# Cross-attention and quantised feed-forward on one core: earlier normalisation, q tiles, output passes and input scaling, and the last shares by products

## The chip, the cores and the metric

The kernel runs on one core of a Trainium2 chip. The metric is device time in microseconds (us). TensorE is called PE below, VectorE DVE, ScalarE ACT, GpSimd POOL, and SP is SyncE's queue, from which every DMA of this kernel is issued.

## The reference, cut to what matters

There are 16 sequences of 256 tokens and 512 features, 16 heads of 32 features, and one layer:

```python
x = x + xattn(layernorm(x), ctx, ctx, wq, wk, wv, wo_w, wo_b)
x = x + ffn(layernorm(x), W_in, b_in, W_out, b_out)

# xattn: q from the normalised x, k and v from ctx; rope on q and k
qp, kp, vp = rope(q @ wq.T), rope(k @ wk.T), v @ wv.T
scores = where(|i - j| <= 128, qh @ kh.T * sqrt(32), -inf)
out = (softmax(scores) @ vh) @ wo_w.T + wo_b
# ffn: W_in and W_out rounded to 8 bit by row, x and hidden to 16 bit by one scale over the tensor
out = quant16(gelu(quant16(x) @ quant8(W_in) + b_in)) @ quant8(W_out) + b_out
```

## The kernel before, in words

There are three stages. Stage A (0 to about 761 us of the span) is the attention, one step for each of the 16 sequences b. Stages B and C (to the end) are the two feed-forward products; the change leaves them alone. Their 16-bit scale needs the maximum over all of x, so B starts only when A has ended.

All five queues carry hand-written orders in which nothing is reordered at run time; semaphores tie them. Stage A is software-pipelined: step b holds the attention of sequence b, the projections of b+1, the output product, residual and moments of b-1, and the first layer norm's moments of b+2. `has_o`, `has_proj` and `has_xt` say which of these exist; all do in steps 2 to 13.

**First half of a step.** PE computes the scores of 16 heads in pairs (L597, two matmuls a head, two banks in turn). A head's scores wait until DVE has taken the row maxima of the head before last (`row_maxima`, L1063). After each pair comes a projection tile, listed in `tiles`: k half 0; the transposes of x (L526) and k half 1; v of the first 128 tokens; q half 0; q half 1; and v of the second 128 tokens in two halves. On DVE, after each pair, comes what `between` lists: `invert` (the reciprocal of the softmax denominators of b-1, L1104) after pair 0; `xt_rest`; the rotations of k; and `normalise` (L1110) after pair 5, which multiplies the attention output oT of b-1 with the reciprocals. These have to be spread over partitions first: SP sends them to a scratch tensor in HBM and back (`spread_shares`, L349 and L352), and the second transfer signals `share_in`. The transposes of x write the bank that holds the denominators, so they wait for `den_done` of `invert` as well as for `ln1_norm`, which ACT gives after scaling x by the layer norm in place (`norm1`, L820).

**Second half.** DVE negates and splits the maxima (`split_max`, L1068), PE transposes them (L609, once a step), ACT copies them into `q_st` (`max_copy`), and SP copies them on for heads 4 to 15 (`stack_max`). PE then computes transposed scores head by head (L631), ACT takes exp (L864), POOL zeroes what is outside the window (`band`, L1381). Between these heads PE places the 24 matmuls ("passes", L581) of the output product of b-1. After heads 7, 11 and 15, and once more at the end, PE runs a clump: 4 heads' product with v (L645) and their denominators (L658). Transposed scores use three banks, so head 15 waits for the exp of head 12. The next step starts with L597 behind the last clump.

Beside that, ACT splits q and the context into a high part (`split_hi`, `ctx_hi`), POOL computes the low parts (L1358, L1364) between its bands of heads 4 to 11, and DVE does, in this order: `split_max`, the rotations of q, residual and moments of the first half of b-1, `quantise_win` (the rounding of 128 rows of W_in, L1116 to L1123), `ln1` of b+2 (L1024 to L1037, of which 13 instructions work on 2 elements a partition), residual and moments of the second half, and two maxima (`largest`, L1049). SP loads the next rows of W_in (`load_win(b+1)`, L326) when `quantise_win(b)` has ended; behind it in its queue stand the context's load, four groups of stacking DMAs, the store of x1, then the load of x and `spread_shares` of the next step.

Of the kernel before, what the change touches and what calls it, by code (L numbers as in the profile page):

```python
# [20 lines left out]
ALU = mybir.AluOpType  # L21
AX_X = mybir.AxisListType.X
F32 = mybir.dt.float32
# [6 lines left out]
P = 128  # L30
NB, S, D = 16, 256, 512
H, DK = 16, 32
# [32 lines left out]
def constants():  # L65
# [10 lines left out]
    mask = np.concatenate([mask[P:], mask[:P, P:]], 1)  # L76
    hot = np.tile((np.arange(HOT) % NC4 == NC4 - 1).astype(np.float32), (P, 1))
    sel = np.zeros((P, H), np.float32)
    for h in range(H):
        sel[MROW + h, h] = sel[MROW + H + h, h] = 1.0  # L80
    return {"c_rope": rope, "c_mask": mask, "c_sel": sel, "c_hot": hot, "c_ident": np.eye(P, dtype=np.float32)}


def build(nc, t):
# [12 lines left out]
    with ExitStack() as ctx:  # L97
# [22 lines left out]
        for n in ("wk", "wq", "wv", "wo"):  # L120
# [17 lines left out]
        oT = sb("oT", [P, NC4, S], F32, pa)  # L138
        hot = sb("hot", [P, HOT], F32, pa)
        x_ln = sb("x_ln", [P, 2, D], F32, pa)  # L140
        x_res = sb("x_res", [P, 2, D], F32, pa)
# [54 lines left out]

        c_in, rope_in, ident_in, b_out_in = sem("c_in"), sem("rope_in"), sem("ident_in"), sem("b_out_in")
        w_in = {n: sem("in_" + n) for n in ("wk", "wq", "wv", "wo")}
# [16 lines left out]
        st_mm, exp_done, p_ready, pv_mm = sem("st_mm"), sem("exp_done"), sem("p_ready"), sem("pv_mm")  # L215
        den_mm, den_done, den_out, share_in, oT_out, onorm = (
            sem(n) for n in ("den_mm", "den_done", "den_out", "share_in", "oT_out", "onorm"))
        xres_b, res_done = sem("xres_b"), sem("res_done")
# [86 lines left out]
        def _(sp):  # L305
# [33 lines left out]
            def stack_max(b):  # L339

                sp.wait_ge(mT_done, MAX_COPIES * (b + 1))
                for i in range(1, NC4):
                    sp.dma_start(q_st[MROW:P, KC * i:KC * (i + 1)].bitcast(F32),
                                 q_st[MROW:P, 0:KC].bitcast(F32)).then_inc(max_stacked[i - 1], 16)

# [51 lines left out]
            for i in range(2, NC4):  # L397
                stack_part("q", i, 0, part_hi)
                stack_part("q", i, 1, part_hi)
                stack_part("q", i, 2, part_lo)  # L400
            load_ctx(2)

            def step(b, has_o, has_proj, has_xt, has_next):
# [27 lines left out]
            for b in range(NB - 4, NB):  # L431
# [4 lines left out]
                step(b, True, b + 1 < NB, b + 2 < NB, b + 3 < NB)  # L436
            spread_shares(NB - 1)
            load_xres(NB - 1)
# [71 lines left out]
        def _(pe):  # L510
# [189 lines left out]
            def step(b, par, has_c, has_o, has_proj, has_xt):  # L700

                tiles = [[] for _ in range(H // 2)]
                if has_proj:
                    tiles[0] += [lambda: qk_tile(b + 1, "k", 0)]
                    tiles[1] += [lambda: x_transposes(b + 1, 0), lambda: x_transposes(b + 1, 1), lambda: qk_tile(b + 1, "k", 1)]
                    tiles[2] += [lambda: v_tile(b + 1, 0)]
                    tiles[3] += [lambda: qk_tile(b + 1, "q", 0)]
                    tiles[4] += [lambda: qk_tile(b + 1, "q", 1)]
                    tiles[5] += [lambda: v_tile(b + 1, 1, range(2))]
                    tiles[6] += [lambda: v_tile(b + 1, 1, range(2, KC))]  # L710
# [15 lines left out]
                some(4)  # L726
                for n, count in enumerate((1, 2, 2, 3, 1, 1, 1, 0, 1, 1, 1, 0, 1, 1, 0, 0)):
                    scores_t(b, n, has_o, has_proj)
                    some(count)
                    if n in (7, 11, 15):  # L730
                        clump(b, par, n // KC - 1, has_proj)
# [3 lines left out]

            steps(pe, step)
            for _ in o_products(NB - 1, False):
                pass
# [65 lines left out]
        def _(act):  # L804
# [86 lines left out]
            v_copy(0, 0, 1)  # L891
            ctx_hi(1)

            def step(b, par, has_c, has_o, has_proj, has_xt):
                if has_proj:
                    norm1(b + 1)
                if has_proj:
                    xt_lead(b + 1, 0)
                    xt_lead(b + 1, 1)
                    v_copy(b + 1, 1 - par, 0)  # L900
                    split_hi("k", b + 1)
                if has_o:
                    ot_lead(b - 1, 0, has_proj)
                    ot_lead(b - 1, 1, has_proj)
                if has_proj:
                    v_copy(b + 1, 1 - par, 1)
                max_copy(b, 0, slice(0, 2))
                max_copy(b, 0, slice(2, KC))
                for n in range(H):
                    softmax_exp(b, n)  # L910
                    if n == 4 and has_proj:
                        split_hi("q", b + 1)
                    if n == 8 and has_xt:
                        ctx_hi(b + 2)
                    if n == 12:
                        oT_copy(b, 0)
                    if n == 13 and has_o:
                        centre(b - 1, 0)
                if has_o:
# [101 lines left out]
        def _(dve):  # L1021
# [151 lines left out]
            def step(b, par, has_c, has_o, has_proj, has_xt):  # L1173

                between = {p: [] for p in range(H // 2)}
                if has_o:
                    between[0] += [lambda: invert(b - 1)]
                    between[5] += [lambda: normalise(b - 1, 0), lambda: normalise(b - 1, 1)]
                if has_proj:
# [12 lines left out]
                if has_o:  # L1192
                    residual(b - 1, 0)
                    ln2_moments(b - 1, 0)
                quantise_win(b)
                if has_xt:
                    ln1(b + 2)
                if has_o:
                    residual(b - 1, 1)
# [10 lines left out]
            invert(NB - 1)  # L1210
            normalise(NB - 1, 0)
            normalise(NB - 1, 1)
            ot_rest(NB - 1, 0)
# [242 lines left out]
```

## Time and profile before

| | us |
|---|---|
| median of 3 runs | 1254.26 (1252.21 to 1255.16) |
| the profiled execution | 1251.07 |
| its span | 1249.3 |
| PE busy | 1138.1 (91%) |
| DVE busy | 981.0 (79%) |
| ACT busy | 639.6 (51%) |
| POOL busy | 366.4 (29%) |

The span is the stretch that the profile covers; 1.8 us of the execution lie around it. Busy time is summed over instructions, and matmuls overlap, so PE's share overstates its work. The chain of work that ended last runs 38% over PE, 31% over DVE, and 24% is issue time.

### The profile page before, as it was taken

How to read it: one execution, taken by the hardware profiler on the slowest of the kernel's cores; microseconds unless marked ns; L12 is line 12 of the kernel's file. 1: busy time of each engine (PE TensorE's matmuls, PEld its weight loads, DVE VectorE, ACT ScalarE, POOL GpSimd, SP SyncE). 2: the span in 40 equal slices, each digit the busy share in tenths (PEclk: the TensorE clock that was granted, in tenths of full speed). 3: DMA queues.
4: the chain of work that ended last, by engine and by line, in shares of the span. 5: the costliest groups of instructions: out<-in, count | busy, mean ns of one | idle time of the engine just before them, and what ended most of it. 6: DMA issues, size and time to landing. Idle time of an engine off the chain costs nothing.

```text
span 1249.3 us, 23318 instructions
## 1 busy us (share of the span) xinstructions
PE 1138.1 (91%) x7776; PEld 759.7 (61%) x7776; DVE 981.0 (79%) x2527; ACT 639.6 (51%) x1000; POOL 366.4 (29%) x540
## 2 busy tenths in 40 slices
PE   5889999999999899999999665999999979999997
PEld 5767777787777688677768443444444434444443
DVE  6769989989988988988899545666666678888885
ACT  5254355335435534543553243555655458777774
POOL 1136336344533634453363220000000030112220
PEclk9889999999999999999999787999999989999999
DMA  8453575566456447545644711455554400567762
GB/s 270 110 143 106 158 178 137 139 183 155 108 161 177 131 134 194 140 120 164 177 119 114 218 56 69 160 206 198 208 188 143 152 0 35 186 224 249 219 207 92
DMA packets 96055, 191.44 MB, mean 153 GB/s; under 512 B 13392, under 2 KB 24912, under 8 KB 95952
## 3 DMA queue, kind: packets, MB, share of 16 engines
q1 hardware_dynamic: 95952, 190.14, 51.5%
q8 instruction: 56, 0.92, 0.3%
q14 instruction: 47, 0.39, 0.1%
HBM read 89.43 MB, written 44.04 MB: 107 GB/s over the span
## 4 chain that ended last, share of the span: by engine, by line
PE 38%; DVE 31%; issue 24%; DMA 3%; SPq 2%; ACT 2%; POOL 0%; DVEq 0%; ACTq 0%; POOLq 0%
PE bank L792 17%; DVE bank L1063 6%; PE bank L514 4%; PE bank L515 4%; PE bank L516 4%; DVE bn L1024 3%; PE bank L597 2%; DVE roped L1089 2%; DVE neg_max L1104 2%; DVE rt L1086 2%; DVE row_max L1063 2%; DVE rt L1087 2%; DVE x_res L1056 1%; PE bank L526 1%; PE bank L581 1%
## 5 line engine op out<-in xcount | busy, mean ns | idle before, releaser
L1063 DVE CUSTOM_DVE_ANT_0 bank<-bank,mask 128x256 f32<-128x256 f32 x512 | 201.4, 454 | 54.6 <-PE bank L597 48.0
L792 PE MATMUL bank<-wout_int,g_hi 128*128 128x512 bf16 x512 | 195.8, 382 | 8.8 <-DVE g_lo L1336 8.7
L792 PE MATMUL bank<-wout_int,g_lo 128*128 128x512 bf16 x512 | 195.6, 382 | 0.0
L761 PE MATMUL bank<-qT_hi,win_int 128*128 128x512 bf16 x512 | 194.2, 379 | 1.4 <-DVE qT_lo L1254 1.4
L761 PE MATMUL bank<-qT_lo,win_int 128*128 128x512 bf16 x512 | 194.1, 379 | 0.0
L864 ACT ACTIVATE probs<-bank 128x512 f32<-128x512 f32 x256 | 142.4, 603 | 52.8 <-PE bank L631 48.3
L1381 POOL TENSOR_SCALAR_AFFINE_SELECT probs<-probs 128x256 f32<-128x256 f32 x256 | 109.1, 430 | 82.9 <-ACT probs L864 78.6
L1336 DVE TENSOR_TENSOR g_lo<-h_int,g_hi 128x512 f16<-128x512 f32 x128 | 104.3, 815 | 35.6 <-ACT g_hi L991 34.3
L597 PE MATMUL bank<-k_st,q_st 96*128 96x256 f32 x512 | 98.4, 306 | 25.7 <-DVE row_max L1063 19.3
L1374 POOL TENSOR_TENSOR x_res<-x_res,wo_b 128x512 f32<-128x512 f32 x32 | 42.0, 1332 | 243.9 <-DMA x_res<-in_x 231.1
L964 ACT ACTIVATE h_ring<-bank,b_in,g_scale 128x512 f32<-128x512 f32 x96 | 73.5, 778 | 75.2 <-PE bank L761 58.1
L1278 DVE TENSOR_REDUCE hmax<-h_ring 128x512 f32 (+1 forms) x96 | 63.4, 682 | 60.6 <-ACT h_ring L964 58.6
L631 PEld LDWEIGHTS bank<-q_st,k_st 128*128 128x128 f32 x512 | 90.3, 193 | 31.8 <-issue 13.6
L597 PEld LDWEIGHTS bank<-k_st,q_st 96*128 96x128 f32 x512 | 76.8, 195 | 50.1 <-DVE row_max L1063 30.8
L631 PE MATMUL bank<-q_st,k_st 128*128 128x256 f32 x512 | 104.1, 294 | 3.1 <-DMA q_st<-q_st 2.0
L991 ACT CAST g_hi<-h_int 128x512 f16<-128x512 f32 x128 | 78.7, 615 | 39.6 <-PE bank L792 31.4
L792 PEld LDWEIGHTS bank<-wout_int,g_hi 128*128 128x128 f16 x512 | 50.4, 98 | 71.4 <-issue 11.2
L1421 POOL TENSOR_TENSOR xq<-xq,b_out 128x512 f32<-128x512 f32 x32 | 48.3, 1540 | 154.5 <-DMA xq<-x_scratch 147.7
L761 PEld LDWEIGHTS bank<-qT_hi,win_int 128*128 128x128 bf16 x512 | 50.1, 98 | 62.3 <-DVE qT_lo L1254 3.1
L792 PEld LDWEIGHTS bank<-wout_int,g_lo 128*128 128x128 f16 x512 | 50.4, 98 | 61.0 <-issue 1.6
L761 PEld LDWEIGHTS bank<-qT_lo,win_int 128*128 128x128 bf16 x512 | 50.1, 98 | 59.2
L514 PE MATMUL bank<-cT_hi,wk_hi 128*128 128x256 f32 x256 | 74.5, 291 | 12.6 <-DVE cT_lo L1141 12.6
(146 smaller groups left out, 2666.2 us busy)
## 6 DMA issues: line engine op xcount, KB each, us to landing
hidden_scratch<-h_ring SPq DMA_DIRECT2D x96, 256.0 KB, 2.0
h_ring<-hidden_scratch SPq DMA_DIRECT2D x96, 256.0 KB, 3.0
k_st<-k_hi SPq DMA_DIRECT2D x128, 128.0 KB, 2.5
q_st<-q_hi SPq DMA_DIRECT2D x128, 128.0 KB, 2.4
xq<-x_scratch SPq DMA_DIRECT2D x16, 1024.0 KB, 6.2
x_ln<-in_x SPq DMA_DIRECT2D x16, 512.0 KB, 4.5
ctx_raw<-in_ctxT SPq DMA_DIRECT2D x16, 512.0 KB, 4.9
k_st<-k_lo SPq DMA_DIRECT2D x64, 128.0 KB, 2.7
```

Source lines behind the costliest of these rows:

```text
L514: pe.matmul(out, l_hi, r_hi, start=first, stop=False)
L597: mm = pe.matmul(ring[n % 2][:, qb * S:(qb + 1) * S], q_st[0:MROW, n, qb * P:(qb + 1) * P], k_st[0:MROW, n], start=True, stop=True)
L631: mm = pe.matmul(third[n][:, kb * S:(kb + 1) * S], k_st[:, n, kb * P:(kb + 1) * P], q_st[:, n], start=True, stop=True)
L761: mm = pe.matmul(bank[f % 4][:], win_int[:, c, f * P:(f + 1) * P], part[:, par, c], start=c == 0 and part is qT_hi, stop=c == KC - 1 and p ...
L792: mm = pe.matmul(bank[4 * par + u][:], part[:, f % 4, u * P:(u + 1) * P], wout_int[:, f], start=f == 0 and part is g_hi, stop=f == FC - 1 ...
L864: act.activation(probs[:, n % SLOTS].rearrange("p k q -> p (k q)"), third[n][:], ACT.Exp, scale=SCORE_SCALE).then_inc(exp_done, 1)
L964: act.activation(dst, bank[f % 4][:], ACT.Gelu, bias=b_in[:, f:f + 1], scale=g_scale[:, f:f + 1]).then_inc(gelu_done, 1)
L991: act.copy(g_hi[:, f % 4], h_int[:, f % 4]).then_inc(ghi_done, 1)
L1063: dve.tensor_tensor_reduce(sc, sc, mask[:, (1 - qb) * P:(1 - qb) * P + S], 1.0, NEG, ALU.add, ALU.max, row_max[:, qb, n:n + 1]).then_inc(m ...
L1278: dve.tensor_reduce(hmax[:, bass.ds(FC * n + f, 1)], src, AX_X, ALU.max, apply_absolute_value=True).then_inc(hmax_done, 1)
L1336: dve.tensor_tensor(g_lo[:, f % 4], h_int[:, f % 4], g_hi[:, f % 4], ALU.subtract).then_inc(glo_done, 1)
L1381: pool.affine_select(out=far, in_=far, compare_op=ALU.is_ge, fill=0.0, base=1 - P, pattern=[[0, 2], [1, P]], channel_multiplier=1).then_in ...
```

## The change

- PE: `tiles` holds q's two halves at places 2 and 3 and v's first tile at place 4 (before: v, q, q). The 16 passes left after the transposes of the maxima are all issued before head 8; before, 12 were, and 4 followed later.
- ACT: `norm1(b+2)` stands after the exp of head 11 of step b (before: `norm1(b+1)` at the start of a step, the same scaling half a step later), `ctx_hi` after head 7 and not 8, `v_copy` of the first tile behind the copies of oT's high part, and the first copy of oT and `centre` behind the exp of head 15 (before: behind 12 and 13).
- DVE: `normalise` after pair 4 and not 5, and `ln1(b+2)` ahead of `quantise_win(b)`.
- SP: `stack_max` starts after the first copy of the maxima, and reads one head's copy four times.
- The last sequence's shares go by PE: 4 products with a constant selection matrix (`pick`, a new 256 KB load) spread the reciprocals into two banks, and DVE multiplies from there. The last `spread_shares` is gone.

```diff
@@ sync @@
-                sp.wait_ge(mT_done, MAX_COPIES * (b + 1))
+                sp.wait_ge(mT_done, MAX_COPIES * b + 1)
-                                 q_st[MROW:P, 0:KC].bitcast(F32)).then_inc(max_stacked[i - 1], 16)
+                                 q_st[MROW:P, 0:1].bitcast(F32).to_broadcast([P - MROW, KC, S])).then_inc(max_stacked[i - 1], 16)
             load_ctx(2)
+            sp.dma_start(pick[:], t["c_pick"]).then_inc(pick_in, 16)
...
-            spread_shares(NB - 1)
             load_xres(NB - 1)
@@ tensor, step @@
-                    tiles[2] += [lambda: v_tile(b + 1, 0)]
-                    tiles[3] += [lambda: qk_tile(b + 1, "q", 0)]
-                    tiles[4] += [lambda: qk_tile(b + 1, "q", 1)]
+                    tiles[2] += [lambda: qk_tile(b + 1, "q", 0)]
+                    tiles[3] += [lambda: qk_tile(b + 1, "q", 1)]
+                    tiles[4] += [lambda: v_tile(b + 1, 0)]
-                for n, count in enumerate((1, 2, 2, 3, 1, 1, 1, 0, 1, 1, 1, 0, 1, 1, 0, 0)):
+                for n, count in enumerate((1, 2, 2, 3, 2, 2, 2, 2, 0, 0, 0, 0, 0, 0, 0, 0)):
@@ tensor, behind the steps @@
+            pe.wait_ge(pick_in, 16)
+            pe.wait_ge(den_done, NB)
+            for half in range(2):
+                pe.wait_ge(oT_out, 2 * NB - 1 + half)
+                for a in range(2):
+                    mm = pe.matmul(pv_bank[half][:, a * S:(a + 1) * S], pick[:, 2 * half + a], den_r, start=True, stop=True)
+                mm.then_inc(share_mm, 1)
@@ scalar @@
             ctx_hi(1)
+            norm1(1)
             def step(b, par, has_c, has_o, has_proj, has_xt):
-                if has_proj:
-                    norm1(b + 1)
                 if has_proj:
                     xt_lead(b + 1, 0)
                     xt_lead(b + 1, 1)
-                    v_copy(b + 1, 1 - par, 0)
                     split_hi("k", b + 1)
                 if has_o:
                     ot_lead(b - 1, 0, has_proj)
                     ot_lead(b - 1, 1, has_proj)
                 if has_proj:
+                    v_copy(b + 1, 1 - par, 0)
                     v_copy(b + 1, 1 - par, 1)
...
-                    if n == 8 and has_xt:
+                    if n == 7 and has_xt:
                         ctx_hi(b + 2)
-                    if n == 12:
-                        oT_copy(b, 0)
-                    if n == 13 and has_o:
-                        centre(b - 1, 0)
+                    if n == 11 and has_xt:
+                        norm1(b + 2)
+                oT_copy(b, 0)
+                if has_o:
+                    centre(b - 1, 0)
@@ vector @@
-                    between[5] += [lambda: normalise(b - 1, 0), lambda: normalise(b - 1, 1)]
+                    between[4] += [lambda: normalise(b - 1, 0), lambda: normalise(b - 1, 1)]
...
-                quantise_win(b)
                 if has_xt:
                     ln1(b + 2)
+                quantise_win(b)
...
-            normalise(NB - 1, 0)
-            normalise(NB - 1, 1)
+            for half in range(2):
+                dve.wait_ge(share_mm, half + 1)
+                part = oT[:, 2 * half:2 * half + 2].rearrange("p i t -> p (i t)")
+                dve.tensor_tensor(part, part, pv_bank[half][:], ALU.mult).then_inc(onorm, 1)
```

## Rows read from the trace of the kernel before

**Rows 1.** Busy time by stretch, one whole step (stretch, length, busy and count per engine, PEclk, DMA).
```profile
304.25:347.81 43.56, 41.23 (x355) 33.26 (x351) 38.65 (x117) 19.59 (x35) 20.18 (x32) 1.00 0.56 148
```
**Rows 2.** Timeline of PE: the transposes of the maxima in steps 1 and 14.
```profile
110.46 0.44 PE L609 MATMUL bank<-ident,neg_max 128*128 128x128 f32 x2 [0.39 <-DVE neg_max L1070]
...
680.48 0.44 PE L609 MATMUL bank<-ident,neg_max 128*128 128x128 f32 x2 [0.39 <-DVE neg_max L1070]
```
**Rows 3.** Timeline of DVE, second half of that step, and the next row maximum.
```profile
335.35 0.69 DVE L1116 TENSOR_REDUCE w_s<-w_raw 128x1 f32<-128x512 f32 x1
...
338.32 0.69 DVE L1024 BATCH_NORM_STATS2 bn<-x_ln 128x6 f32<-128x512 f32 x1
...
340.44 0.41 DVE L1034 TENSOR_SCALAR veps<-mv 128x2 f32<-128x2 f32 x1
...
345.45 0.16 DVE L1037 SCALAR_TENSOR_TENSOR nmr<-mv,rstd 128x2 f32<-128x2 f32 x1
...
349.18 0.42 DVE L1063 CUSTOM_DVE_ANT_0 bank<-bank,mask 128x256 f32<-128x256 f32 x1
```
**Rows 4.** Timeline of DVE: one form of short instruction in step 0 and in that step.
```profile
76.27 0.16 DVE L285 TENSOR_TENSOR nt_t<-rstd 128x2 f32<-128x2 f32 x1
...
343.35 0.67 DVE L285 TENSOR_TENSOR nt_t<-rstd 128x2 f32<-128x2 f32 x1
```
**Rows 5.** Timeline of POOL beside it.
```profile
343.28 0.73 POOL L1364 TENSOR_TENSOR cT_lo<-ctx_raw,cT_hi 128x256 fp32r<-128x256 f32 x1
```
**Rows 6.** Busy time by stretch, POOL alone.
```profile
337.47:344.02 6.55, 6.55 (x13) 1.00 0.46 106
```
**Rows 7.** Timeline of ACT: scaling of x; exps of heads 9 to 11 and 14, 15.
```profile
305.44 1.52 ACT L820 ACTIVATE x_ln<-x_ln,nmr,rstd 128x512 f32<-128x512 f32 x2
...
339.88 1.57 ACT L864 ACTIVATE probs<-bank 128x512 f32<-128x512 f32 x3
...
344.22 1.09 ACT L864 ACTIVATE probs<-bank 128x512 f32<-128x512 f32 x2
```
**Rows 8.** Timeline of PE: third clump, fourth clump, next step's scores.
```profile
343.36 1.07 PE L645 MATMUL bank<-probs,v_sb 128*32 128x256 f32 x16
...
345.94 1.07 PE L645 MATMUL bank<-probs,v_sb 128*32 128x256 f32 x16 [0.32 <-POOL probs L1381]
...
347.81 0.74 PE L597 MATMUL bank<-k_st,q_st 96*128 96x256 f32 x4
```
**Rows 9.** Timeline of PE, first half: the transposes of x.
```profile
308.77 1.06 PE L526 MATMUL bank<-ident,x_ln 128*128 128x128 f32 x8 [0.47 <-DVE neg_max L1104]
```
**Rows 10.** Timeline of DVE, first half: head 10, `normalise`.
```profile
322.97 0.43 DVE L1063 CUSTOM_DVE_ANT_0 bank<-bank,mask 128x256 f32<-128x256 f32 x1 [0.58 <-PE bank L597]
...
324.46 1.29 DVE L1110 TENSOR_TENSOR oT<-oT,probs 128x512 f32<-128x512 f32 x2
```
**Rows 11.** Timeline of SP: second transfer of the shares, load of W_in.
```profile
317.71 0.58 SPq L352 DMA_DIRECT2D probs<-den_scratch  x1
...
344.22 0.59 SPq L326 DMA_DIRECT2D w_raw<-in_winT  x1
```
**Rows 12.** The second transfer's line, all 16, issue to landing.
```profile
DMA to landing us min/median/max: 3.5/3.7/5.3
```
**Rows 13.** Timeline of DVE, step 15.
```profile
719.84 0.69 DVE L1110 TENSOR_TENSOR oT<-oT,probs 128x512 f32<-128x512 f32 x1 [7.71 <-DMA probs<-den_scratch]
```
**Rows 14.** Chain of waits, end of stage A (start, length, what).
```profile
744.98 1.70 DMA den_scratch<-neg_max
746.70 3.85 DMA probs<-den_scratch
...
753.42 4.62 PE bank L581 x12
```
**Rows 15.** Busy time by stretch with the granted clock (PEclk, third from the end).
```profile
743.10:746.60 3.50, 0.03 (x4) 0.00 (x0) 1.76 (x1) 0.30 (x1) 0.00 (x0) 1.00 0.11 37
746.60:756.90 10.30, 3.48 (x8) 2.81 (x9) 2.59 (x4) 1.14 (x2) 2.50 (x2) 0.50 0.29 103
```

More of the change, by code:

```diff
@@ L77, in constants @@
     hot = np.tile((np.arange(HOT) % NC4 == NC4 - 1).astype(np.float32), (P, 1))
+    row, col = np.arange(P)[:, None], np.arange(P)[None, :]
+    pick = np.stack([row == DK * (col // DK) + i for i in range(NC4)], 1).astype(np.float32)
     sel = np.zeros((P, H), np.float32)
@@ L80, in constants @@
         sel[MROW + h, h] = sel[MROW + H + h, h] = 1.0
-    return {"c_rope": rope, "c_mask": mask, "c_sel": sel, "c_hot": hot, "c_ident": np.eye(P, dtype=np.float32)}
+    return {"c_rope": rope, "c_mask": mask, "c_sel": sel, "c_hot": hot, "c_pick": pick, "c_ident": np.eye(P, dtype=np.float32)}
 def build(nc, t):
@@ L139, in build @@
         hot = sb("hot", [P, HOT], F32, pa)
+        pick = sb("pick", [P, NC4, P], F32, pa)
         x_ln = sb("x_ln", [P, 2, D], F32, pa)
@@ L194, in build @@
         share = probs[:, 0:2].rearrange("p n k q -> p (n k q)")
-        c_in, rope_in, ident_in, b_out_in = sem("c_in"), sem("rope_in"), sem("ident_in"), sem("b_out_in")
+        c_in, rope_in, ident_in, pick_in, b_out_in = (sem(n) for n in ("c_in", "rope_in", "ident_in", "pick_in", "b_out_in"))
         w_in = {n: sem("in_" + n) for n in ("wk", "wq", "wv", "wo")}
@@ L215, in build @@
         st_mm, exp_done, p_ready, pv_mm = sem("st_mm"), sem("exp_done"), sem("p_ready"), sem("pv_mm")
-        den_mm, den_done, den_out, share_in, oT_out, onorm = (
-            sem(n) for n in ("den_mm", "den_done", "den_out", "share_in", "oT_out", "onorm"))
+        den_mm, den_done, den_out, share_in, share_mm, oT_out, onorm = (
+            sem(n) for n in ("den_mm", "den_done", "den_out", "share_in", "share_mm", "oT_out", "onorm"))
         xres_b, res_done = sem("xres_b"), sem("res_done")
```

## The prediction

> **What bounds the kernel now.** I read the page's parts 1, 2 and 4 first. No engine fills the span, and the chain changes between PE and DVE, so the answer lies in the steps. Stage A, the only one touched, repeats: the transposes of the maxima of steps 1 and 14 lie 570.02 us apart [rows 2], 13 steps of 43.85. I then read one step, 304.25 to 347.81, by engine. PE is busy 41.23 of 43.56, DVE 38.65, ACT 19.59, POOL 20.18 [rows 1]. The reader is to see two things.
>
> In the second half, DVE runs through `quantise_win` (335.35 to 338.3), `ln1` (338.32 to 345.61) and the rest without a stop until 349.18, where the next step's first row maximum starts [rows 3]. PE has issued those scores at 347.81 [rows 8], 1.4 us earlier. In the first half, the transposes of x wait, at 308.77, for DVE's reciprocal and not for ACT's scaling, which ended at 306.96 [rows 7, 9]. So DVE closes the step and PE has about one microsecond in hand.
>
> POOL has no gap from 337.47 to 344.02: 13 instructions in 6.55 us [rows 6], so its bands and low parts run back to back.
>
> **What the order of `ln1` does.** The new place starts it where `quantise_win` started, at 335.35. Its length isn't fixed. The same kind of short instruction takes 0.16 us in step 0, where POOL stood still, and 0.67 us here [rows 4]; it ends at 344.02, and POOL's instruction beside it at 344.01 [rows 5]. So the short ones go one per POOL instruction while POOL is full. Its first four instructions (`bn_stats`, `bn_aggr`) take 2.1 us, from 338.32 to the first short one at 340.44 [rows 3], wherever they stand. Moved up, the short ones start near 337.47 and 13 of them meet POOL's 13 instructions, so `ln1` ends near 344.05: 8.7 us instead of 7.3. Bounds: 7.3 (end 342.65) if only the old number is held, 8.7 as taken. The Trainium skill (SBUF — State Buffer, "SBUF: two separate sides") says that one shared port pair is an exclusive lock between VectorE and GpSimd, held for a whole instruction, by two-port modes or by two SBUF inputs. By that rule the short instructions of `ln1` block wherever POOL is full, as the rows show (0.67 against 0.16), which gives the 8.7; the rule speaks against moving these ops into POOL's fullest stretch.
>
> **What ACT does with it.** ACT ends the exp of head 11 at 341.45 (339.88 + 1.57 [rows 7]), now about 0.6 sooner since no passes lie between. Then it has to scale x, and waits for all of `ln1`: from 344.1, for 1.52 us [rows 7], to 345.6. Behind that wait stand the exps of heads 12 to 15. One is 0.5 us (3 in 1.57), so they run from 345.6 to 347.65; before they ended at 345.31 [rows 7]. Two parties wait for them:
> - PE. Head 15's scores need the bank of head 12, whose exp ends at 346.15. PE has nothing from about 342.2 (second clump and heads 12 to 14 done) to 346.25: 4 us. Then 0.25 for head 15, 1.87 for the third clump (345.94 to 347.81 is one clump [rows 8]), 0.4 for the weights' transposes (an estimate: 343.36 + 1.87 to 345.94, less its 0.32 of waiting), and 1.87 for the fourth: next scores at 350.65 against 347.81, +2.85.
> - POOL's last band needs the exp of head 15 and is done near 348.3, which is sooner.
>
> DVE is ready at 350.0 (344.05, 2.35 for `quantise_win`, an estimate from its 2.95 beside a full POOL [rows 3], and the 3.57 from 345.61 to 349.18) and starts 0.6 behind the scores, at 351.25 against 349.18: +2.1. PE's transposes of x stand behind k's half tile: the gap of 0.47 ahead of 308.77 began at 308.3, 4.05 behind the step's start, so they come at 350.65 + 4.05 = 354.7 against 308.77 + 43.56 = 352.33 [rows 9]. **+2.3 us a step.** Scaling x half a step sooner gives nothing against it, as `den_done` was the later wait [rows 9].
>
> **`normalise` after pair 4.** DVE waits 0.58 us for head 10's scores [rows 10]; 1.29 us of `normalise` [rows 10] now lies there, so the maximum of head 10 starts 0.7 later. Before, `normalise` covered the time in which PE computed v's last piece, behind which the scores of head 14 stand. Now DVE is idle there, and I take it that 0.3 of the 0.7 comes back: +0.4. Below that lies -0.6 (the gap filled, all kept), above +0.7.
> The shares may also be late. `load_win(b+1)` waits for `quantise_win(b)`, which now ends at 346.4 instead of 338.3; the DMA issued at 344.22 [rows 11] comes 2.2 later and all behind it on SP too (two stacking pairs, store of x1, load of x, `spread_shares`). The second transfer, issued at 317.71 [rows 11], lands 3.7 later [rows 12], at 321.4, 1.0 before the new place of `normalise` (322.4); with both shifted by 2.2 to 2.3 it is about even, and in steps where SP is later (a landing took up to 5.3 [rows 12]) DVE waits. I take +0.2. Together **+0.6 a step**.
>
> **The rest.** q's tiles before v's: the same 12 or 24 matmuls and the same length, and q isn't rotated before the second half: 0. Twelve passes ahead of head 8 become 16 ahead: they partly fill PE's wait ahead of the first clump and are missing later, where PE now waits for ACT anyway: 0, between -0.5 and +0.5 a step. `stack_max` earlier by one copy (0.5 us): 0, between -0.5 and 0. `pick` and `norm1(1)` in the prologue: 0.7 us of queue, covered. In step 0 `ln1` is short (0.16 [rows 4]) and there is no `normalise`; I take +0.7 for steps 0 and 1 together.
> Step 15: `normalise` waited 7.71 us for the shares [rows 13], behind the loads of xq. Two more heads' maxima (2 x 0.77) now come behind this wait: +1.5. Its second half has no `norm1` and is freed of two ACT copies ahead of the last exps: -0.8, between -1.2 and 0.
> The last shares: two DMAs of 1.70 and 3.85 us [rows 14] and the wait behind them go. In come 4 products of 256 columns. The trace has none of that form; a clump's 16 of the same type, four side by side, take 1.87 us [rows 8], so one alone is near 0.47: 1.9 in all (3.8 at half clock), and the first half's multiply overlaps the second's products. From 744.98 that is 747.0 and one multiply of 0.7, 747.7. Before, the shares had landed at 750.55 and the two multiplies took 1.29 [rows 10], 751.9: -4.2. The first 12 passes behind it took 4.62 us [rows 14], 3.5 of them at half clock [rows 15]; with PE's gap cut to some 2 us they would take 2.9, and I keep 1.1 of this 1.7, as POOL's bias of x is then due: -5.3 in all. Ends: -2.4 (products at half clock) and -5.9.
>
> **The clock.** In this step the granted clock is 1.00, 2.4 GHz [rows 1]. After 743.10, with nothing issued for 3.5 us, it is 0.50, 1.2 GHz, and stays so for 10.3 us, 3.5 of them behind the return of the work at 753.42 [rows 14, 15]. The new gap of 4 us in each step is as long. A fall costs half of the 3.5 us, 1.75, if full clock comes back as it did there; up to 5 if it lasts for all 10.3. I take 7 falls in 13 steps, 12 us. The skill (TensorE: Matmul & The Clock Gate, "HAM oscillation — how this bites in real kernels") warns of PE gaps of some 3 us in each round of a loop. By it nearly all 13 steps would fall: 23 us.
>
> **The sum.** 13 x (2.3 + 0.6) = 37.7; + 0.7 + 1.5 - 0.8 - 5.3 = 33.8; with the clock 45.8. On the profiled execution's 1251.07 (span 1249.3 and 1.8 around it) that is 1296.9; the median stands 3.2 higher: **1300**. Without any fall of the clock 1288.
>
> **Rivals.**
> A. `ln1` keeps its 7.3 us, ends at 342.65, and the wait is 1.4 shorter: 0.9 + 0.6 a step, 19.5 - 3.9 (the four single terms) = 15.6: 1270. For it: it is the length that the rows have. Against: in it the last ones, at 0.16 [rows 3], were free of POOL, and in the new place none is. With half of it, 1285.
> B. The exps aren't held, since `ln1` ends before 341: only `normalise` costs, 6.5 - 3.9: 1257. For it: with all short ones at 0.16 and 0.04 between them, as in step 0 [rows 4], it would take 2.1 + 2.6 = 4.7 us and end at 340.1. Against: POOL would have to stand still.
> C. Faster. `ln1` is done before ACT asks, and DVE, which closes the step, wins the 0.58 us idle ahead of head 10 each time: -0.58 x 13 - 3.9 = -11.4: 1243. It decides at one point: the end of `ln1` before the exp of head 11 (341). Against it are the held instructions, as for B.
> D. The clock falls in every step and for long, 13 x 3.5: 1334.
>
> **How the numbers follow.** Forecast with some falls or none, 1285 to 1315: 0.48; A up to 1285: 0.20; D, above 1315: 0.10; B 0.09, of which 0.05 within 0.2% (2.5 us, what a measurement here can tell from no change); C 0.13. So slower 0.82, same 0.05, faster 0.13. The range leaves out C, part of B and the far end of D: 1255 to 1325.
>
> **What would show it.** Right: `norm1` of steps 0 to 13 waits for DVE's last `ln1` instruction; short `ln1` instructions of 0.3 to 0.7 us nearly all through; a gap of 3 to 5 us on PE ahead of head 15; the next step's first scores 2.9 us later from the transposes of the maxima; stretches of clock 0.5 inside steps 1 to 13; in step 15 heads 10 and 11 behind the shares; at the end of stage A, 5 us less. Wrong: the exp of head 12 following that of head 11 within 2 us (then B or C), or steps below 44 us.

## The result and the profile after

The changed kernel takes 1315.03 us, the median of 4 runs (1309.34 to 1318.56), against 1253.24 (1250.35 to 1255.16) for the kernel before in the same job: ratio 1.0491, 95% interval 1.0443 to 1.0539. The profiled execution took 1312.53, its span is 1310.8. The forecast was 1300, in the right direction and 15 us short.

Busy time by stretch, one whole step from next scores to next scores, and below it the end of the step before it, cut by clock (columns as in [rows 1]; PEclk is the third number from the end; matmuls that overlap are counted once in these figures and in the page's):

```profile
326.61:374.55 47.94, 42.56 (x355) 33.58 (x352) 40.07 (x117) 20.18 (x35) 20.79 (x32) 0.96 0.51 138
316.90:320.40 3.50, 0.48 (x5) 0.27 (x3) 3.22 (x9) 1.85 (x3) 1.60 (x3) 1.00 0.57 130
320.40:323.80 3.40, 3.20 (x26) 1.70 (x30) 2.85 (x7) 3.34 (x7) 1.63 (x4) 0.51 0.43 142
```

Against [rows 1] the step has the same counts and is 4.4 us longer, of which 1.3 are PE's busy time (42.56 against 41.23), with the mean clock at 0.96 instead of 1.00. The rest is waiting. The second and third lines show a stretch in which PE does nearly nothing, and the 3.4 us at half clock right behind it.

Timeline of PE: the transposes of the maxima in steps 1 and 14 (they answer to [rows 2]), and between them the second half of the step that begins at 304.13 (to [rows 8]):

```profile
111.11 0.44 PE L612 MATMUL bank<-ident,neg_max 128*128 128x128 f32 x2 [1.15 <-DVE neg_max L1080]
...
316.41 0.97 PE L634 MATMUL bank<-q_st,k_st 128*128 128x256 f32 x6
320.60 0.80 PE L634 MATMUL bank<-q_st,k_st 128*128 128x256 f32 x2 [3.22 <-ACT probs L874]
321.33 1.94 PE L648 MATMUL bank<-probs,v_sb 128*32 128x256 f32 x16
...
324.74 1.07 PE L648 MATMUL bank<-probs,v_sb 128*32 128x256 f32 x16
...
326.61 0.73 PE L600 MATMUL bank<-k_st,q_st 96*128 96x256 f32 x4
...
694.35 0.44 PE L612 MATMUL bank<-ident,neg_max 128*128 128x128 f32 x2 [1.14 <-DVE neg_max L1080]
```

From 111.11 to the transposes of step 14 at 743.59 lie 632.48 us, 13 steps of 48.65: +4.80 a step, 62.4 in all, the whole of the loss. PE waits 3.22 us for an exp ahead of head 15, and the clump behind it takes 1.94 us where the next one, at full clock, takes 1.07.

Timeline of ACT, the same stretch (to [rows 7]):

```profile
313.46 2.07 ACT L874 ACTIVATE probs<-bank 128x512 f32<-128x512 f32 x4 [0.93 <-PE bank L634]
318.55 1.52 ACT L830 ACTIVATE x_ln<-x_ln,nmr,rstd 128x512 f32<-128x512 f32 x2 [3.03 <-DVE nmr L1047]
319.97 2.06 ACT L874 ACTIVATE probs<-bank 128x512 f32<-128x512 f32 x4
```

Timeline of DVE: `ln1` ahead of `quantise_win`, the next row maximum, and `normalise` of the next step (to [rows 3, 4, 10]); below it POOL beside `normalise`:

```profile
310.07 0.69 DVE L1034 BATCH_NORM_STATS2 bn<-x_ln 128x6 f32<-128x512 f32 x1
...
312.18 0.21 DVE L1044 TENSOR_SCALAR veps<-mv 128x2 f32<-128x2 f32 x1
...
313.48 0.65 DVE L288 TENSOR_TENSOR nt_t<-rstd 128x2 f32<-128x2 f32 x1
...
318.55 0.69 DVE L1126 TENSOR_REDUCE w_s<-w_raw 128x1 f32<-128x512 f32 x1
...
327.30 0.43 DVE L1073 CUSTOM_DVE_ANT_0 bank<-bank,mask 128x256 f32<-128x256 f32 x1 [2.79 <-PE bank L600]
...
344.06 1.89 DVE L1120 TENSOR_TENSOR oT<-oT,probs 128x512 f32<-128x512 f32 x2
```
```profile
343.51 3.72 POOL L1370 TENSOR_TENSOR k_lo<-roped,k_hi 128x256 fp32r<-128x256 f32 x4 [1.98 <-ACT k_hi L820]
```

ACT reaches the scaling at 315.5, waits 3.03 us for the last instruction of `ln1`, and the four last exps stand behind it. `ln1` runs from 310.07 to 318.51. At 327.30 DVE, which in the kernel before was the one to close the step, waits 2.79 us for PE: the step is now closed by the chain ln1, scaling, exp of head 12, head 15, clumps.

The groups of PE by line, whole span, first of the kernel before and then of the changed one (busy, mean ns | idle before, releasers):

```profile
L631 PE MATMUL bank<-q_st,k_st 128*128 128x256 f32 x512 | 104.1, 294 | 3.1 <-DMA q_st<-q_st 2.0 <-ACT q_st L857 0.7 <-ACT probs L864 0.4
```
```profile
L634 PE MATMUL bank<-q_st,k_st 128*128 128x256 f32 x512 | 101.5, 304 | 47.3 <-ACT probs L874 46.2 <-ACT q_st L867 0.7 <-DMA q_st<-q_st 0.5
```

In the whole span PE waited 0.4 us for exps in the kernel before, and 46.2 in the changed one, of which 42.0 are the 13 gaps ahead of head 15 in steps 1 to 13 (3.22 each, 3.42 in step 1).

### The profile page after: what moved, and what is told of

It reads as the page before. It is cut to its first block, busy times and chain, and to the rows that moved or that the text cites. A ratio compares the mean times of both kernels' runs of the same rounds, so it can differ in the third digit from the quotient of the medians.

```text
span 1310.8 us, 23288 instructions
## 1 busy us (share of the span) xinstructions
PE 1161.8 (89%) x7740; PEld 765.1 (58%) x7784; DVE 999.3 (76%) x2527; ACT 640.1 (49%) x1000; POOL 379.4 (29%) x540
## 4 chain that ended last, share of the span: by engine, by line
PE 39%; DVE 30%; issue 25%; ACT 2%; DMA 2%; SPq 1%; DVEq 0%; POOL 0%; POOLq 0%; ACTq 0%
PE bank L802 16%; DVE bank L1073 6%; PE bank L648 4%; DVE roped L1099 3%; PE bank L661 3%; PE bank L517 3%; PE bank L518 3%; PE bank L519 3%; PE bank L600 3%; DVE rt L1096 3%; DVE rt L1097 3%; DVE bn L1034 2%; DVE row_max L1073 2%; DVE nt_t L288 2%; PE bank L634 1%
## 5 line engine op out<-in xcount | busy, mean ns | idle before, releaser
L802 PE MATMUL bank<-wout_int,g_hi 128*128 128x512 bf16 x491 | 187.6, 382 | 8.6 <-DVE g_lo L1348 8.5
L771 PE MATMUL bank<-qT_hi,win_int 128*128 128x512 bf16 x489 | 185.4, 379 | 0.0
L874 ACT ACTIVATE probs<-bank 128x512 f32<-128x512 f32 x256 | 137.2, 598 | 32.9 <-PE bank L634 28.1
L634 PE MATMUL bank<-q_st,k_st 128*128 128x256 f32 x512 | 101.5, 304 | 47.3 <-ACT probs L874 46.2
L634 PEld LDWEIGHTS bank<-q_st,k_st 128*128 128x128 f32 x512 | 83.2, 195 | 79.8 <-ACT probs L874 52.8
L1386 POOL TENSOR_TENSOR x_res<-x_res,wo_b 128x512 f32<-128x512 f32 x32 | 45.5, 1442 | 240.2 <-DMA x_res<-in_x 230.9
L820 ACT CAST k_hi<-roped 128x1024 fp32r<-128x1024 f32 x15 | 15.8, 1051 | 153.6 <-DVE roped L1099 153.6
```

The source lines that it names most:

```text
L634: mm = pe.matmul(third[n][:, kb * S:(kb + 1) * S], k_st[:, n, kb * P:(kb + 1) * P], q_st[:, n], start=True, stop=True)
L771: mm = pe.matmul(bank[f % 4][:], win_int[:, c, f * P:(f + 1) * P], part[:, par, c], start=c == 0 and part is qT_hi, stop=c == KC - 1 and p ...
L802: mm = pe.matmul(bank[4 * par + u][:], part[:, f % 4, u * P:(u + 1) * P], wout_int[:, f], start=f == 0 and part is g_hi, stop=f == FC - 1 ...
L874: act.activation(probs[:, n % SLOTS].rearrange("p k q -> p (k q)"), third[n][:], ACT.Exp, scale=SCORE_SCALE).then_inc(exp_done, 1)
```

## The experiments

The columns of this table are means over steps 1 to 13, in us from the step's transposes of the maxima: end of the last exp, next step's first scores on PE, next step's first row maximum on DVE, and the whole step. Beside them stand the length of `ln1` and how often in these steps the granted clock fell to 0.50. All are read from the profiled executions.

| kernel | time | ln1 | last exp | scores | maximum | step | falls |
|---|---|---|---|---|---|---|---|
| before | 1253 | 7.35 | 16.02 | 18.51 | 19.53 | 43.85 | 0 |
| change | 1315.0 | 8.45 | 17.90 | 22.77 | 23.46 | 48.65 | 13 |
| e1_scale_back | 1291.5 | 8.50 | 14.95 | 19.18 | 20.17 | 46.88 | 7 |
| e2_scale_alone | 1295.9 | 8.04 | 18.62 | 22.05 | 22.74 | 47.27 | 12 |
| e3_filler | 1291.0 | 8.49 | 17.92 | 21.00 | 21.70 | 46.89 | 0 |
| e4_normalise_alone | 1266.6 | 7.29 | 15.91 | 18.40 | 19.44 | 44.60 | 0 |
| e5_win_behind | 1267.8 | 8.45 | 14.92 | 19.15 | 20.14 | 45.01 | 0 |
| e7_passes_alone | 1258.4 | 7.70 | 16.15 | 18.64 | 19.83 | 44.20 | 0 |
| e8_ln1_later | 1248.8 | 6.27 | 16.08 | 18.57 | 19.26 | 43.72 | 1 |
| e9_ln1_later_orig | 1291.2 | 4.66 | 16.02 | 18.51 | 21.53 | 46.98 | 9 |
| e10_pool_late | 1289.6 | 5.28 | 16.80 | 19.29 | 19.98 | 46.72 | 11 |

### e1_scale_back: the scaling at its old place

```diff
@@ scalar, on the changed kernel @@
-            norm1(1)
+                if has_proj:
+                    norm1(b + 1)          # at the step's start
...
-                    if n == 11 and has_xt:
-                        norm1(b + 2)
```

> The changed kernel with one part undone: ACT scales x at the start of the step again (norm1(b+1)); ln1 ahead of quantise_win, normalise after pair 4, passes, tiles and the product shares stay. Theory (the exps of heads 12 to 15 are held behind ACT's wait for ln1, and the gap on PE drops its clock): both go; no PE gap over 2 us ahead of head 15, clock 1.00 through steps 1 to 13, steps of 44.5 to 45.3 us (DVE closes them 0.6 later since ln1 is longer, and normalise costs 0.5 to 1), 1258 to 1270 us. Rival (normalise and the late shares, behind the late load of W_in on SP, are the main cost): these stay, so steps stay above 47 us and the time above 1295.

Measured: 1291.5 (1291.09 to 1292.39), ratio 1.0303 (1.0286 to 1.032). 24 us came back, not 45 to 57, so neither forecast was met: the first put the time under 1270, the rival above 1295. The held exps are gone (last exp 14.95), and the next maximum comes 0.64 behind that of before. But the steps are still 3 us longer. What `normalise` waited for in this kernel (sum in us, times), from the answer for its line:

```profile
  DMA probs<-den_scratch: 20.7, 14
```

14 steps waited for the shares: step 15 for 10.9 us, and 13 others for 9.8 together. In the changed kernel only step 15 did. A late wait had hidden another: as soon as the exps were in time, the shares weren't.

### e5_win_behind: e1 with the load of W_in behind the store of x1

```diff
@@ sync, on e1_scale_back @@
-                    load_win(b + 1)
                 if has_o:
                     store_x1(b - 1)
+                if has_proj:
+                    load_win(b + 1)
```

> e1 (the changed kernel with x scaled at the step's start) and load_win(b+1) moved behind the store of x1 in SP's order, so that nothing on SP waits for quantise_win but this load. e1 left steps of 46.8 us where 45 was expected, and in it DVE waited for the shares in 14 steps, 20.7 us. Theory (quantise_win's late end holds SP's queue through load_win, and so the shares): the waits for the shares fall to the last steps' 12 us or less, the second transfer is issued 2 us sooner after the transposes of the maxima (32 to 33 instead of 34.5), steps of 45 to 45.8 us, 1268 to 1280 us. Rival (the shares are late for another reason, the later denominators or slower DMAs): the issue and the waits stay, within 4 us of 1291.5.

Measured: 1267.76 (1266.51 to 1270.34), ratio 1.0129 (1.0112 to 1.0146): another 24 us less, and 0.2 below the range expected. Over steps 1 to 13 the second transfer of the shares is issued 31.6 us behind the transposes of the maxima instead of 34.4.

```profile
L1120 DVE TENSOR_TENSOR oT<-oT,probs x30: 685/742/1226, 105.0 to 738.3; 128x512 f32<-128x512 f32 x30
...
  DMA probs<-den_scratch: 10.6, 1
```

One wait is left, step 15's. So `load_win`, whose wait for the later `quantise_win` stood in SP's queue ahead of the shares, made 24 us of e1's time. The waits were 10 us of it. The 7 falls of the clock in e1, behind gaps of PE of 1.4 to 2.3 us ahead of the scores that DVE's late maxima held, went with them. At the 1.77 us that e3 gives for a fall at another place they are 12 us more; in e1 itself the steps with a fall are 1.3 us longer than those without, which makes 9. The rest was not separated.

### e2_scale_alone: only ln1 first and the scaling behind head 11

```diff
@@ scalar and vector, on the kernel before @@
-                    norm1(b + 1)          # at the step's start
+                    if n == 11 and has_xt:
+                        norm1(b + 2)
...
-                quantise_win(b)
                 if has_xt:
                     ln1(b + 2)
+                quantise_win(b)
```

> The kernel before with only ln1 ahead of quantise_win and x scaled after the exp of head 11. Theory: the whole wait is made by these two lines; gap on PE ahead of head 15 of 3 us or more, clock 0.50 in each of steps 1 to 13, steps of 47 to 48.5 us, 1290 to 1315 us. Rival (normalise and the shares are the main cost): steps below 45 us and under 1270.

Measured: 1295.85 (1293.1 to 1298.34), ratio 1.0331 (1.0312 to 1.035), +42.6, as expected. The two moves by themselves give the late exps, the falls (12) and +3.42 a step, seven tenths of the loss. But PE's gap is 2.3 us here in most steps (3.02 in step 1), under the 3 expected, and the clock did not fall in every step: with the same gap of 2.3 it fell in 9 of 11, and not in steps 3 and 8.

### e3_filler: the changed kernel with work for PE in the gap

```diff
@@ tensor, scores_t of head 15, on the changed kernel @@
+                if n == H - 1 and has_proj and has_xt:
+                    for _ in range(12):
+                        pe.matmul(q_bank[0][:], w_hi["wv"][:, 0, 0:P], w_hi["wv"][:, 0], start=True, stop=True)
```

The 12 products go into a bank that is free at that time, and nothing reads them.

> The changed kernel with 12 more matmuls (128x512, constant weights, into a free bank, results unused) on PE ahead of head 15's scores in steps 0 to 13: some 2.8 us of work in the 3.2 us gap. Theory (the gap costs by itself and again by the fallen clock): clock 1.00 through steps 1 to 13, steps 1.1 to 2 us shorter than the 48.65 of the change, 1288 to 1302 us. Rival (the fallen clock is hidden behind DVE): within 3 us of 1315, or slower where the filler comes late.

Measured: 1291.0 (1290.08 to 1292.66), ratio 1.0301 (1.0284 to 1.0318). More work, 24 us less. Timeline of PE around the gap, and busy time by stretch of steps 1 to 13:

```profile
314.30 2.92 PE L634 MATMUL bank<-wv_hi 128*128 128x512 f32 x12
317.71 0.50 PE L638 MATMUL bank<-q_st,k_st 128*128 128x256 f32 x2 [0.49 <-ACT probs L878]
318.15 1.07 PE L652 MATMUL bank<-probs,v_sb 128*32 128x256 f32 x16
```
```profile
112.68:722.22 609.54, 570.77 (x4707) 455.89 (x4707) 525.93 (x1522) 259.27 (x442) 271.88 (x416) 1.00 0.52 139
```

The exps end as late as in the change (17.92 against 17.90), but the clump takes 1.07 us instead of 1.94 and the clock is 1.00 throughout. The next scores come 1.77 us sooner: this is what a fall costs a step, and 13 of them make 23.0.

### e4_normalise_alone

```diff
@@ vector, on the kernel before @@
-                    between[5] += [lambda: normalise(b - 1, 0), lambda: normalise(b - 1, 1)]
+                    between[4] += [lambda: normalise(b - 1, 0), lambda: normalise(b - 1, 1)]
```

> The kernel before with only normalise moved from pair 5 to pair 4. Theory: it costs 0.4 us a step for the lost cover, 0.6 more since it now meets POOL's k_lo (1.89 us instead of 1.29 in the trace of the change), and 1.5 in step 15: 1258 to 1268. Rival (it fills DVE's 0.58 us ahead of head 10): 1243 to 1250.

Measured: 1266.62 (1264.94 to 1268.69), ratio 1.0111 (1.0094 to 1.0128), +0.75 a step; the next row maximum isn't later (19.44), so all of it lies in the first half. The time is in the range expected, the step less than the 1.0 forecast. The mean length of a `normalise` instruction is 957 ns for 744, 0.43 a step, which leaves 0.3 for the lost cover. DVE waited for the shares in three of these steps, 1.1 us together.

### e7_passes_alone

```diff
@@ tensor, on the kernel before @@
-                for n, count in enumerate((1, 2, 2, 3, 1, 1, 1, 0, 1, 1, 1, 0, 1, 1, 0, 0)):
+                for n, count in enumerate((1, 2, 2, 3, 2, 2, 2, 2, 0, 0, 0, 0, 0, 0, 0, 0)):
```

> The kernel before with only the output passes bunched ahead of head 8. Theory: DVE closes the step, PE has a microsecond in hand: no change, 1251 to 1255 us. Rival: bunching fills PE's wait ahead of the first clump and shortens steps by up to 0.5 us: 1245 to 1250; or leaves a gap later that drops the clock: above 1258.

Measured: 1258.39 (1257.22 to 1259.64), ratio 1.0048 (1.0035 to 1.0061). It costs 6 us, 0.35 a step. The theory of no change missed, and the rival's figure, above 1258, was met for another reason, as the clock never fell. The tuple, which counts the passes behind each head, moves five of them ahead of head 8, not four: in the kernel before 11 of the 16 stood there and 5 later. At 0.235 us each (the distance of their starts in the timeline) five are 1.17 us, PE's wait ahead of the first clump was 0.80, and the clump starts 0.34 later (7.10 against 6.76). `ln1` takes 7.70 instead of 7.35 and ends 0.29 later; the next maximum is 0.30 later. That POOL's bands, pushed back, hold more of `ln1` is how I read it; it wasn't separated further.

### e11_tiles_alone and e12_scale_end

```diff
@@ tensor and scalar, e11 on the kernel before @@
-                    tiles[2] += [lambda: v_tile(b + 1, 0)]
+                    tiles[2] += [lambda: qk_tile(b + 1, "q", 0)]      # v's first tile at place 4, its copy behind oT's
@@ scalar, e12 on the kernel before @@
-                    norm1(b + 1)          # at the step's start
+                if has_xt:
+                    norm1(b + 2)          # behind the exp of head 15
```

> The kernel before, only q's two tiles ahead of v's first one (and its copy on ACT behind those of oT). Theory: the same matmuls in another order, no consumer earlier: 1251 to 1256. Rival (v's copy now stands behind two oT copies and holds the bank for v's second tile): 1256 to 1262.

> The kernel before, x scaled half a step sooner as in the change, but behind the exp of head 15 and not that of head 11. Theory (the loss of the change lies in the exps queued behind the wait for ln1; the transposes of x wait for the reciprocals, not for the scaling): no exp waits, 1250 to 1256, no gain and no loss. Rival (the copies of oT and of W_in's transposes, now 1.5 to 1.8 us later on ACT, hold PE's banks): 1257 to 1275. Rival (scaling sooner lets the transposes of x run sooner): under 1250.

Measured: 1253.61 (1250.66 to 1256.91), ratio 1.0004 (0.999 to 1.0017), and 1253.98 (1250.43 to 1258.34), ratio 1.0004 (0.9989 to 1.0018). Both are nothing. In e12 x is scaled a half step sooner at no cost, and gains nothing, because the transposes of x still wait for the reciprocal. Groups of PE by line:

```profile
L526 PE MATMUL bank<-ident,x_ln 128*128 128x128 f32 x128 | 17.0, 276 | 7.5 <-DVE neg_max L1105 7.1 <-issue 0.2
```

So the sooner scaling was worth nothing, and with the order of `ln1` as before its place behind the exp of head 15 costs nothing; its place behind head 11 is what held the last exps in e2 and in the change.

### e6_tail_alone

The kernel before with the last `spread_shares` replaced by the 4 products (the diff's part "tensor, behind the steps", with the load of `pick` and the two multiplies).

> The kernel before with only the last sequence's shares by products. Theory: 4 to 5 us less at the end of stage A and nothing else: 1248 to 1250 us. Rival (the new load, or the lower clock behind the products, gives it back): 1252 or more.

Measured: 1248.52 (1245.3 to 1251.85), ratio 0.997 (0.996 to 0.998). The one part that gains, 3.7 us.

### e10_pool_late: fewer POOL instructions beside ln1

```diff
@@ gpsimd, on the kernel before @@
-                    if n in (8, 9, 10, 11) and has_xt:
-                        ctx_lo(b + 2, n - 8)
+                    if n == H - 1 and has_xt:
+                        for c in range(KC):
+                            ctx_lo(b + 2, c)
```

> The kernel before, POOL's four low parts of the context (ctx_lo) moved from behind the bands of heads 8 to 11 to behind the band of head 15. Theory (DVE's short instructions go one per POOL instruction): with four of POOL's 13 instructions gone from under ln1 it takes 5.0 to 6.5 us instead of 7.3, its short ones 0.16 to 0.3 us where POOL stands still. Rival (the length belongs to the instructions or to ACT's scaling): 7.0 to 7.6 as before. The time itself may be longer, 1255 to 1290, since k's first product of the next step waits for the low parts.

Measured: 1289.62, one run, so its time is worth less than the others'. `ln1` takes 5.28 us, 2.07 less, though it isn't touched. One form of its short instructions by line, in the kernel before and in this one:

```profile
L285 DVE TENSOR_TENSOR nt_t<-rstd 128x2 f32<-128x2 f32 x48 | 16.8, 349 | 1.6
```
```profile
L285 DVE TENSOR_TENSOR nt_t<-rstd 128x2 f32<-128x2 f32 x48 | 9.2, 193 | 1.7
```

The same instruction, 349 ns against 193: its length is POOL's doing. The Trainium skill's rule of the exclusive lock (SBUF — State Buffer, "SBUF: two separate sides") fits this.

The 36 us of loss have another source than the one expected, as far as this trace tells. PE waits little for k's first product. But the load of the context stands in SP's queue ahead of the shares and waits for the low parts, and the second transfer of the shares is issued 36.8 us behind the transposes of the maxima, against 32.3 before. DVE waits for it in 12 of the 13 steps, 16.9 us together, and PE then has gaps of 1.6 to 4.5 us with 11 falls behind them. No run took this apart.

### e8_ln1_later and e9_ln1_later_orig: ln1 the other way

```diff
@@ vector, on e6_tail_alone @@
                 quantise_win(b)
-                if has_xt:
-                    ln1(b + 2)
                 if has_o:
                     residual(b - 1, 1)
                     ln2_moments(b - 1, 1)
+                if has_xt:
+                    ln1(b + 2)
+                if has_o:
                     largest(b - 1, 0)
```

e8 has the bunched passes of e7 as well; e9 has the passes as before.

> The kernel before with the product shares, the passes bunched ahead of head 8, and on DVE ln1(b+2) moved the other way: behind residual and moments of the second half, ahead of the two maxima. Theory (short instructions of ln1 go one per POOL instruction while POOL is full): ln1 starts 2.3 us later, more of it lies behind POOL's last band, it takes 5.5 to 6.5 us instead of 7.3, and since DVE closes the step, steps are 0.5 to 1 us shorter until PE's scores bound: 1237 to 1245 us. Rival (ln1's length is its own): 7.3 us still, 1247 to 1251 us by the shares alone.

> The kernel before, with the last shares by products, ln1 of b+2 behind residual and moments of the second half, and the passes where they were (1,1,1,0,1,1,1,0,... after the first four heads). Theory (the costs of the parts add up): the bunched passes cost 6.1 us when alone, the same order of ln1 with them gave 1248.8; without them 1240 to 1245. Rival (with a shorter ln1, PE closes every step and what DVE gains beyond that is lost): 1246 to 1249, and row 0's first maximum follows PE's first scores by 0.7 us in both.

Measured: e8 1248.77 (1245.73 to 1250.84), ratio 0.9969 (0.9958 to 0.998); e9 1291.24 (1290.59 to 1293.52), ratio 1.0304 (1.0287 to 1.0322). With `ln1` where POOL has nearly finished it takes 6.27 us in e8, as expected, but the time is a miss, 4 us above the range: the steps are 0.13 us shorter than before and not 0.5 to 1. That buys back what the bunched passes cost, and e8 ends level with e6. e9 is a plain miss, 46 to 51 us off: I had added parts and forgotten what the order was for. Timeline of DVE in one step of e9:

```profile
360.39 0.69 DVE L1067 TENSOR_TENSOR x_res<-bank,x_res 128x512 f32<-128x512 f32 x1 [4.63 <-PE bank L585]
...
365.09 0.16 DVE L289 TENSOR_TENSOR nt_t<-rstd 128x2 f32<-128x2 f32 x1
```

The residual needs the last passes of the output product, and these come late when they are spread. Before, `ln1` stood ahead of it and filled that wait; now DVE stands idle for 4.63 us, then runs `ln1` at its free length (0.16 for a short one), and the next maximum comes 2.0 late. Then the clock, in e9's stretches:

```profile
373.00:376.40 3.40, 3.40 (x18) 3.40 (x17) 1.30 (x3) 0.48 (x1) 0.00 (x0) 0.50 0.60 147
368.70:371.75 3.05, 1.13 (x6) 0.63 (x5) 3.05 (x11) 0.00 (x0) 0.00 (x0) 1.00 0.84 207
```

## Why the prediction was right, and where it was short

**`ln1` in the fullest stretch of POOL.** Right. 8.45 us on average for my 8.7 (7.35 before), 8.44 in the step shown. ACT waited 3.03 us; `quantise_win` took 2.43 for my 2.35.

**The held exps.** Right in mechanism, and near in size. PE's gap was 3.22 for my 4. Without the clock (e3_filler) the next scores come at 21.00 from the transposes of the maxima, against my 350.65 - 329.4 = 21.2, and the next maximum is 2.17 later than before, against +2.1.

**`normalise` after pair 4, +0.6.** Nearly right in size, wrong in one of its two terms. In the change the part of a step behind the first maximum is 0.87 longer (25.19 against 24.31), where my terms put 0.8 (0.6, and the 0.2 between +2.1 and +2.3). But the shares were late in none of steps 1 to 13: DVE itself was later. Instead `normalise` met POOL's low parts of k and takes 1.89 us for two instead of 1.29. By line, in the changed kernel:

```profile
L1120 DVE TENSOR_TENSOR oT<-oT,probs 128x512 f32<-128x512 f32 x30 | 27.6, 959 | 9.7 <-DMA probs<-den_scratch 9.7
```

Before, the mean was 744 ns; 2 x 0.215 = 0.43 a step, which leaves 0.44 for the lost cover, my 0.4 (0.3 in e4). The late shares are real, but of the runs of these moves only e1 shows more than 0.1 us a step of them, where the exps are in time and `load_win` stands ahead of the shares (e1 against e5).

**The passes, 0.** Wrong when they stand alone, 0.35 a step (e7), and inside my bounds of -0.5 to 0.5. The three parts by themselves, 3.42 (e2) + 0.75 (e4) + 0.35 (e7), make 4.52 of the change's 4.80; in time e2, e4, e7, e11 and e6 add up to 58.7 us of 61.8. The other moves (`stack_max`, `ctx_hi`, the later copies of oT) were not run alone; 3.1 us are left for them and for what the parts do to each other. In e3_filler, where they are in too, the step is +3.04 for my 2.9 in all, so there is little room for them in my own terms.

**The clock, 7 falls for 12 us.** This is the step that failed, as the term that was mis-sized. The clock fell in 13 of 13 steps, and a fall cost 1.77, by e3 against the change; I had 1.75 for each, but 7 of them. 13 x 1.77 = 23.0 against 12: 11 of the 15 us. The same work by the rule of the Trainium skill (TensorE: Matmul & The Clock Gate, "HAM oscillation — how this bites in real kernels") had been 13 falls and 23 us, so its count was right here, and my halving had nothing behind it: the rows hold one gap, in which the clock fell after 3.5 us with nothing issued. Falls in only part of the steps do occur, but at shorter gaps: 13 of 13 steps fell at 3.2 to 3.4 us, 9 of 11 at 2.3 (e2), 4 of 8 at 1.4 (e1) and 9 of 13 at 1.3 (e9). Rival D had all 13, but priced them at 3.5; the low stretches are 3.4 us in ten steps and 6.8 in three, 4.2 on average, and 1.77 of that is lost.

**Step 15.** DVE waited 9.72 us for the shares for 7.71 [rows 13], and the interval from step 14's transposes to step 15's grew by 1.6 (46.23 for 44.61) against my 1.5. Its second half was to gain 0.8 and lost 0.7 (18.83 us from its transposes to the reciprocals, 18.10 before). The place is the passes: the first clump starts at 7.66 for 6.20 from the transposes. The text on the change and the prediction have 12 passes ahead of head 8 going to 16; the tuple has 11. In this step PE had no wait ahead of the clump for them to fill, and five more at 0.235 us are 1.17. The other 0.3 is the clock, which is at half for 1.7 us behind these transposes, against 1.1 before. Timeline of PE at this place, before and after:

```profile
731.29 1.07 PE L645 MATMUL bank<-probs,v_sb 128*32 128x256 f32 x16
```
```profile
797.48 1.07 PE L648 MATMUL bank<-probs,v_sb 128*32 128x256 f32 x16
```

**The last shares, -5.3.** -4.2 from the start of the reciprocals to stage B (23.3 us against 27.5). Timelines of PE and DVE, and one stretch with its clock:

```profile
810.51 1.97 PE L745 MATMUL bank<-neg_max,pick 128*128 128x256 f32 x8 [1.93 <-issue]
814.67 0.47 PE L584 MATMUL bank<-wo_hi,t_hi 128*128 128x512 f32 x1 [2.20 <-ACT t_hi L851]
```
```profile
812.51 0.69 DVE L1224 TENSOR_TENSOR oT<-oT,bank 128x512 f32<-128x512 f32 x1 [0.17 <-PE bank L745]
```
```profile
815.40:818.80 3.40, 3.40 (x9) 2.67 (x8) 0.00 (x0) 0.00 (x0) 2.38 (x2) 0.50 0.00 0
```

The products took 1.97 (I had 1.9) and the last multiply ended 2.8 behind the end of the reciprocals (2.7). What failed is the 1.1 for the passes: the clock fell there too, behind gaps of 1.93 and 2.20 us, shorter than before, when PE had waited 10.3 us.

**The sum.** On the profiled executions, 1312.53 against my 1296.9 are 15.6 us: 13 x 0.98 in the steps (0.85 of it the clock), 0.1 at steps 14 and 15, and 2.6 from step 15's second half on (1.5 in the half step, 1.1 in the passes), 15.4 together.

Rivals A, B and C needed `ln1` to end sooner than it did: it ended 14.40 us behind the transposes of the maxima, 3.0 behind the exp of head 11. B's 6.5 us for `normalise` is 0.5 a step where my own term was 0.6, so B should have stood at 1258 and not 1257. Both better versions, e6_tail_alone and e8_ln1_later, leave the exps alone; they are 3.7 and 3.4 us under the kernel before, and not told apart from one another.

## What to carry to other kernels

Before a step is moved up, look at what will stand behind its wait: here two multiplications of x, moved half a step ahead of their use, put four exps and thus a third engine behind a chain of thirteen tiny instructions. A gap that recurs in each round of a loop at about the length after which the clock once fell is to be priced as a fall in every round: here 13 of 13 at 3.2 us, 9 of 11 at 2.3, and about half or more at 1.3 to 1.4. Price the moves together as well as alone: a late wait hides another (e1), and an order that looks idle may be what fills somebody's wait (e9).

## What the runs showed of the hardware that was not expected

- The clock can fall without one long gap. In e9 the longest gap of PE in that place was 1.3 us, and from 368.70 to 371.75 it was busy for 1.13 of 3.05 us; at 373.00 the granted clock went to 0.50 for 3.4 us, in 9 of 13 steps. The Trainium skill (TensorE: Matmul & The Clock Gate, "A second HAM failure mode: psum-queue depth-cycling") tells of such falls from frequent short idle times, and the trace agrees.
- Twelve useless matmuls in the gap of 3.2 us are worth 1.8 us each time, since PE then runs what follows at 2.4 GHz.
- An instruction on 2 elements a partition takes 0.16 us on DVE where POOL stands still (e9, at 365.09), and 0.65 where POOL is full (the change, at 313.48). POOL in `ln1`'s stretch of the changed kernel:

```profile
312.18:318.51 6.33, 6.21 (x12) 1.00 0.69 155
```

  12 POOL instructions lie beside the 13 short ones. A pair of `TENSOR_TENSOR` on 512 elements is held as well: 1.89 us beside POOL's low parts, 1.29 without.
